# Cross attention with its scores on 64 by 64 tiles of the array, over key rows interleaved by part

## The reference

```python
x = x + _L1_xattn_ref(_layernorm(x, axis=-1), ctx_1024, ctx_1024, mask_Bx1xSxS2_bk0, ...)

def _L1_xattn_ref(queries, keys, values, mask, W_q, W_k, W_v, W_proj, b_proj):
    Q = (queries @ W_q.T).reshape(b, sq, N_HEADS, D_HEAD).transpose(0, 2, 1, 3)
    K = (keys @ W_k.T).reshape(b, -1, N_HEADS, D_HEAD).transpose(0, 2, 1, 3)
    V = (values @ W_v.T).reshape(b, -1, N_HEADS, D_HEAD).transpose(0, 2, 1, 3)
    scores = jnp.einsum('bhqd,bhkd->bhqk', Q, K) / scale
    scores = jnp.where(mask, scores, NEG_INF)
    attention = jax.nn.softmax(scores, axis=-1)
    heads_out = jnp.einsum('bhqk,bhkd->bhqd', attention, V)
    ...
    out = heads_out @ W_proj.T + b_proj
```

## Time and profile before

| | |
|---|---|
| median of 3 runs | 2487.47 us (2486.67 to 2489.14) |
| the profiled execution | 2501.07 us, span 2499.3 us, mean granted PE clock 0.971 |
| PE busy | 2236.3 us (89%) |
| DVE, ACT, POOL busy | 1650.0 (66%), 1243.2 (50%), 808.3 us (32%) |
| the stage's loop over batches: first K00, last addition of the output | 386.27, 732.00 us after the span's start |

### The profile page before, as it was taken

The page is one execution under the profiler, slowest core; times in us unless marked ns, Lnnn a source line. Parts: engine busy times, 40 slices in busy tenths (PEclk is TensorE's granted clock), DMA queues, the critical chain, the costliest instruction groups (busy, mean ns, idle before and its releaser), DMA issues. The chain is left out here.

```text
span 2499.3 us, 50978 instructions
## 1 busy us (share of the span) xinstructions
PE 2236.3 (89%) x20593; PEld 1417.7 (57%) x20650; DVE 1650.0 (66%) x3182; ACT 1243.2 (50%) x2071; POOL 808.3 (32%) x660
## 2 busy tenths in 40 slices
PE   6885779999978889999999999699879999998898
PEld 4764445666654555656655666356546555566554
DVE  4987456555548756888888854644576666665577
ACT  2326234555554225555555554566436555563565
POOL 5610052233206112321233300045445455433254
PEclk8998899999989989999999999899999999999999
DMA  3200453423313047676776764133322323220231
GB/s 113 71 7 1 144 136 103 107 78 106 79 66 106 13 118 144 121 133 133 151 146 122 125 113 80 34 102 102 116 67 67 86 69 86 69 67 23 71 96 60
DMA packets 358618, 226.84 MB, mean 91 GB/s; under 512 B 289913, under 2 KB 326610, under 8 KB 358386
## 3 DMA queue, kind: packets, MB, share of 16 engines
q1 hardware_dynamic: 355314, 215.20, 35.5%
q0 software_dynamic: 3072, 8.39, 1.2%
HBM read 114.87 MB, written 0.52 MB: 46 GB/s over the span
## 5 line engine op out<-in xcount | busy, mean ns | idle before, releaser
L3950 POOL TENSOR_TENSOR l2x_rows<-l2x_rows,l2x_one 128x256 f16<-128x256 f32 (+1 forms) x91 | 89.2, 1006 | 379.6 <-DVE l2x_rows L1507 354.5
L100 PE MATMUL PS<-hot 128*128 128x512 f16 x460 | 134.3, 427 | 82.1 <-DVE l0a_g L1119 17.5
L4054 PE MATMUL PS<-l2x_rows,l2x_pth 128*128 128x512 f16 x832 | 200.3, 379 | 1.7 <-DVE l2x_mean L4263 1.7
L3711 DVE CUSTOM_DVE_ANT_0 l1x_junk<-PS,l1x_bias 128x1024 bf16<-128x1024 f32 (+1 forms) x128 | 123.2, 991 | 73.6 <-PE PS L3371 72.7
L4256 DVE TENSOR_TENSOR l2x_pl<-l2x_sc,l2x_ph 128x1664 f16<-128x1664 f32 x64 | 125.1, 1954 | 44.6 <-ACT l2x_ph L4133 43.9
L4151 ACT ACTIVATE l2x_meanT<-PS 128x256 f32<-128x256 f32 x64 | 24.5, 383 | 250.5 <-PE PS L4016 250.5
L4241 DVE CUSTOM_DVE_ANT_0 l2x_sc<-PS,l2x_bias 128x1665 f32<-128x1665 f32 x64 | 120.9, 1889 | 36.3 <-issue 35.0
L3711 DVE CUSTOM_DVE_ANT_0 l3x_junk<-PS,l3x_bias 128x1024 bf16<-128x1024 f32 (+1 forms) x128 | 123.6, 991 | 24.3 <-PE PS L3371 21.6
L4008 PE MATMUL PS<-l2x_kh,l2x_qth 128*128 128x512 f16 (+1 forms) x512 | 131.9, 339 | 1.5 <-issue 1.5
L4008 PE MATMUL PS<-l2x_kh,l2x_qtl 128*128 128x512 f16 (+1 forms) x512 | 131.9, 339 | 0.0
L4008 PE MATMUL PS<-l2x_kl,l2x_qth 128*128 128x512 f16 (+1 forms) x512 | 131.9, 339 | 0.0
(11 more groups left out here) (866 smaller groups left out, 6109.0 us busy)
## 6 DMA issues: line engine op xcount, KB each, us to landing
l2f_unit<-in_L_ffn_units_dram SPq DMA_DIRECT2D x36, 384.0 KB, 3.1
l3f_unit<-in_L_ffn_units_dram SPq DMA_DIRECT2D x34, 384.0 KB, 3.0
l1x_kst<-l1x_kh SPq DMA_DIRECT2D x128, 100.1 KB, 2.2
l3x_kst<-l3x_kh SPq DMA_DIRECT2D x128, 100.1 KB, 2.2
l2x_rows<-in_ctx_dram SPq DMA_DIRECT2D x8, 1536.0 KB
l1x_ctx<-in_ctx_t_dram SPq DMA_DIRECT2D x7, 1601.0 KB, 7.3
l3x_ctx<-in_ctx_t_dram SPq DMA_DIRECT2D x7, 1601.0 KB, 7.0
l1x_kst<-l1x_kl SPq DMA_DIRECT2D x64, 100.1 KB, 2.2
```

The source lines that it names most:

```text
L100: self.nc.tensor.matmul(self.PS[:, bank, :], self.hot[:, 0:P], self.hot[:], start=True, stop=True)
L3711: v.tensor_tensor_reduce(junk[:, slot(it), 0:n], slot_banks(it)[:, 0:n], bias[:, 0 if normed else b % 2, at:at + n], 1.0, LOWEST, ALU.add, ...
L3950: last = nc.gpsimd.tensor_tensor(high[:, at], of[:, at], one[0:p, at].unsqueeze(2).unsqueeze(3).to_broadcast([p, i, NC, P]), ALU.mult)
L4054: nc.tensor.matmul(PS[:, ACC, :], pth[:, u % 2, m, :], rows2[:, b % 2, :, :, m, :], start=(m == 0), stop=False)
```

## The change

A second function, `row_tiled_attention`, is a copy of the first and serves l1x; l3x keeps the old one. What differs for l1x:

- **Key rows.** `kst` has 128 rows instead of 97 for a pair of heads, 64 for each head: rows x, x + 4, x + 8, ... are part x, with x = 0 a constant, 1 and 3 the high, 2 the low keys. The constant rows of both buffers are written once by two DMAs on SP (behind the loads, ahead of the mask's loads) from a row in the spare half of the value buffer; the stack DMAs write every fourth row.
- **Queries.** `qst` has one block of 64 columns for a pair instead of two with a mask: a head's queries stand in its own 64 rows. They are turned by fp16 products with an identity; the pair mask goes.
- **Scores.** `turned(b, m)` makes both banks in one pass: four mask products of 64 by 64 weights and 512 columns, for all 13 m, then 32 score products of 64 by 64 weights and 64 columns, on row half r and column half (a half of the key tile); bank r holds the heads of row half r. It waits for both exponentials of the m before, and at m = 0 for both M items. `values` reads heads 2u + g for g.
- **Mask.** `ON_VECTOR` is empty: DVE adds no mask, and POOL makes no second layout (line 3260 has no counterpart).
- **Maxima.** An A item is two pairs of heads by a quarter of the keys: four products of 401 columns (398 in the last quarter) on four 64 by 64 tiles, and two maxima of 401 on DVE. There are 16 as before. M is two transposes instead of four, and two copies of 1 by 256 on ACT instead of one of 1 by 512.
- **Order.** In the steps that hold both, A now stands ahead of V1, V2 and V3 (and A10 ahead of M0), and M1 moves to the step before the last. ACT and DVE do both exponentials of an m first, then the items of both steps (before: the items of the step before ahead of each exponential). Warm-up is three products for each A item.
- W_proj's rows are laid out for the new order of heads; the mask in columns is no longer an input.

As a diff between the old function and the new one, cut:

```diff
-    ON_VECTOR = list(range(4))
+    ON_VECTOR = list(range(4)) if normed else []
-    A = [("A", u, h) for u in range(R) for h in range(NH)]
+    A = [("A", v, j) for v in range(QV) for j in range(NCH)]
...
-                 [("V", 1, 0), A[2]], [A[3]], [P_, A[4]], [("V", 2, 0), A[5]], [A[6]], [A[7]], [("V", 3, 0), A[8]], [A[9]],
-                 [("M", 0, 0), A[10]], [A[11]], [A[12]], [A[13]], [A[14]], [A[15]], [], [("M", 1, 0)]]
+                 [A[2], ("V", 1, 0)], [A[3]], [P_, A[4]], [A[5], ("V", 2, 0)], [A[6]], [A[7]], [A[8], ("V", 3, 0)], [A[9]],
+                 [A[10], ("M", 0, 0)], [A[11]], [A[12]], [A[13]], [A[14]], [A[15]], [("M", 1, 0)], []]
...
-                for g, part in enumerate((kh, kl, kh)):
-                    sp.dma_start(kst[g * F:(g + 1) * F, b % 2, c * RC + j, :],
+                for x, part in ((1, kh), (2, kl), (3, kh)):
+                    sp.dma_start(kst[x::PARTS, b % 2, c * RC + j, :],
...
+                for a in range(2):
+                    sp.dma_start(kst[0::PARTS, a, :, :], const.unsqueeze(1).to_broadcast([F, R, NK])).then_inc(const_rows, 16)
...
-                for i, at, n in pieces(*halves[j]):
-                    last = nc.tensor.matmul(PS[:, bank + i, 0:n], qst[0:3 * F, b, c, :, :],
-                                            kst[0:3 * F, b % 2, c, at:at + n], start=True, stop=True)
+                at, n = chunks[j]
+                for i in range(2):
+                    for r in range(2):
+                        rows = slice(r * S, (r + 1) * S)
+                        last = nc.tensor.matmul(PS[i * S:(i + 1) * S, bank + r, 0:n], qst[rows, b, 2 * c + i, :],
+                                                kst[rows, b % 2, 2 * c + i, at:at + n], start=True, stop=True)
...
-                def turned(b, m, g):
+                def turned(b, m):
-                            pe.wait_ge(exp_done, e - G2 + 1)
+                            pe.wait_ge(exp_done, e)
-                        pe.wait_ge(row_made, G2 * b + g + 1)
+                        pe.wait_ge(row_made, G2 * (b + 1))
...
+                                    nc.tensor.matmul(PS[at:at + w_, S_BANK + r, :], of_bias[:, m * P + at:m * P + at + w_], one_hot[half, :],
+                                                     start=(x == 0), stop=False, skip_group_check=True)
+                    for u in range(R):
+                        for at, w_ in keys:
+                            for r in range(2):
+                                rows = slice(r * S, (r + 1) * S)
+                                last = nc.tensor.matmul(PS[at:at + w_, S_BANK + r, u * S:(u + 1) * S],
+                                                        kst[rows, b % 2, u, m * P + at:m * P + at + w_], qst[rows, b, u, :],
...
                     for m in range(KT):
+                        turned(b, m)
                         for g in range(G2):
-                            turned(b, m, g)
                             for it in at_step(b, m * G2 + g):
                                 item(it)
...
-                            for it in step_before(b, m * G2 + g):
-                                item(it)
                             exp(b, m, g)
+                        for g in range(G2):
+                            for it in at_step(b, m * G2 + g):
+                                item(it)
```

More of the change, by code:

```diff
@@ L3760, in layer_1_xattn @@
 def layer_1_xattn(k):
-    context_attention(k, "l1x", normed=False, finished=("l0x", "l0a", "l0f"))
+    row_tiled_attention(k, "l1x", normed=False, finished=("l0x", "l0a", "l0f"))
 def layer_3_xattn(k):
@@ L4369, in heads, with heads_by_half @@
         return w.reshape(2, 2, 4, D // H, D).transpose(1, 0, 2, 3, 4).reshape(2, P, D)
+    def heads_by_half(w):
+        return w.reshape(2, 4, 2, D // H, D).transpose(0, 2, 1, 3, 4).reshape(2, P, D)
     def columns(v):
@@ L4415, in laid_out @@
         a[f"L1_xattn_{name}_t"] = a.pop(f"L1_xattn_{name}").T
-    a["L1_xattn_W_proj_t_heads"] = heads(a.pop("L1_xattn_W_proj").T)
+    a["L1_xattn_W_proj_t_heads"] = heads_by_half(a.pop("L1_xattn_W_proj").T)
     both = a.pop("L2_xattn_Wkv")
@@ L4423, in laid_out @@
     a["fside_columns"] = tiled(a["fside_SxS2_0"])
-    a["mask_columns"] = tiled(a["mask_Bx1xSxS2_bk0"][:, 0])
     n = np.arange(D)
```

695 lines of the change are left out of this document (added).

## The result

The changed kernel takes 2505.65 us (median of 5, 2499.12 to 2513.92), beside 2489.14 (2486.67 to 2491.34) for the kernel before: ratio 1.0073, 95% interval 1.0057 to 1.0089. It is slower, by 16.5 us between the medians and 18 by the ratio; 2483.5 was forecast, 2502 was the upper end, and the sign is wrong.

What follows compares the result with a forecast made beforehand. It took PE as the bound, with POOL's fixed 12.0 us from V3's end to K00. Terms -4.4 - 1.9 - 0.5 + 2.9 = -3.9 us off 2487.47 gave 2483.5 (2478 to 2489; 2471 to 2502 with most rivals).

Steps and rivals of the forecast that it cites:

- the price of a score pass: PE's scores of one m: bias 0.22 us plus 8 rounds of 0.032 us, 0.48 us in all.
- T: Time of one score pass on PE: 0.48 us if four tiles run together, 0.95 if two do.
- K00 to V3's end: PE's stretch per batch: -0.82 us in three batches, -0.42 in three with O and P, -0.7 in the first; -4.4 together.
- POOL's cover: After V3, PE reaches the next batch's first T's end in 11.1 to 11.3 us, inside POOL's 12.4: cost 0.
- VectorE: DVE's maximum items: two reductions of 0.50 us, 1.0 an item against 1.15, but 16.0 a batch against 14.6.
- Way in: Up to the first K00: cheaper query turning and copies, first K00 at 384.4 instead of 386.27, -1.9 us.
- End: Last batch, values 0 to the end of values 12: 21.7 us after, 18.8 before, +2.9.
- The chain of 1.81: Last batch: score pass, both exponentials and release follow one another, so one m lasts at least 1.81 us, against 1.56.
- Rival 1: Score passes and maxima: tiles sharing columns, or their weight loads, queue; T 0.95, +27 us, so 2510; chance 0.10.
- Rival 4: Last batch: the clock falls to half, T and values double, +7 us, so 2490; chance 0.06.

Runs made afterwards that it cites:

- grouped_last_tile: The changed kernel with the last key tile's 16 score products of the 64-wide part first, then the 16 of the 1-wide part: 2490.93 us, ratio 1.0006.
- last_key_left_out: The changed kernel without the 1601st key in scores, exponentials and values, so no 1-wide products: 2494.65 us, ratio 1.0029.
- two_bank_pairs: grouped_last_tile with V1, V2, V3 ahead of A2, A5, A8, and the last batch's odd-m scores in two free banks: 2488.53 us, ratio 0.9995.

## Why the prediction was wrong

**The step that failed** is the price of a score pass. T was worked out for a tile of 128 keys and charged 13 times a batch. The words "new ones are charged" put one change of tile size, 0.11 us, to each pass; in m = 12 there are 17 more. Each costs about what was said (0.09 to 0.12), but the number was wrong, and with it the rounds (16 of two products, not 8 of four): the pass takes 2.78 us instead of 0.6. Both facts stood there: 1601 keys leave 65, and the 0.11 was read from the rows. They weren't put together, since the pass was priced from the loop's form and not once for its last turn. What the order of its products alone is worth, by the grouped kernel: 14.5 us of the stage and 15 to 17 of the time. In the profile it is 7.5 us from POOL's start to K00 (1.0 to 1.4 in each of six batches), 2.2 ahead of the last batch and 2.2 in it, 2.2 in K00 to POOL of the two batches in which the clock was lost, and 0.4 in the way in. With it gone the stage is still 1.4 us longer than before, not 3.9 shorter. The other 5.3 are the end (2.2 more than forecast), the way in (1.9), the first batch (0.6) and the stretch ahead of the last batch (0.6).

**Point by point** (what the prediction calls one step of two bias and eight score products is one m, so two steps; its sums use it rightly):
- *K00 to V3's end.* Right, nearly row by row. In the batch of 513.87 (without O and P), from start to start: K00 to values 0 8.05 (8.08 forecast), to values 1 4.15 (4.19), to values 2 3.90 (3.88), to values 4 6.67 (6.6), to values 5 5.41 (5.36), to values 6 1.71 (1.7), to POOL's release 2.89 (2.03 before, +0.85 forecast). Sum -0.74 against -0.82; -0.55 against -0.42 with O and P. The first batch gave -0.1, not -0.7.
- *POOL's cover.* Right as a bound (12.0 in grouped_last_tile and in both kernels without the last key), wrong in what hides under it: "11.1 to 11.3 us" holds only where m = 12 has no change (last_key_left_out: 11.1 in four of six batches), and with the grouped pass it is just under 12.0 (K00 waits 0.2 to 0.3 us for POOL in four batches). In the changed kernel it is 13.1 to 13.5.
- *VectorE.* Right: 1.0 us an item, idle time of PE ahead of V and A items ended by DVE's maxima.
- *Way in.* Not settled to the microsecond: 64.83 after and 64.50 before, but the two kernels with the old way in took 66.06 and 66.54, with the clock at half for other stretches (10.2 us near the start in all but before, where it is 6.8 and 3.4 more at 369; 6.8 more at 355 in those two). So it gave between +0.3 and -1.7, where -1.9 was forecast. The turning products and the copies save what was said (1.95 to 1.07, 2.72 to 1.29 us), but a cost was left out: the query's parts are now written to every fourth fp16 of a row, which DVE does at half the pace. DVE's rows of it before:

```profile
353.22 0.69 DVE L3609 TENSOR_SCALAR l1x_q_high<-l1x_xn 128x1024 f16<-128x1024 f32 x1
...
353.95 1.29 DVE L3611 CAST l1x_v<-l1x_q_high 128x1024 f32<-128x1024 f16 x2
...
355.16 1.22 DVE L3612 SCALAR_TENSOR_TENSOR l1x_v<-l1x_xn,l1x_q_high 128x1024 f32<-128x1024 f32 x1
```

and after, with PE's turning products (line 4104), DVE's copies (4454) and its first maximum (4500):

```profile
340.84 1.32 DVE L4402 TENSOR_SCALAR l1x_v<-l1x_xn 128x1024 f16<-128x1024 f32 x1
...
342.19 1.32 DVE L4403 COPY l1x_v<-l1x_v 128x1024 f16<-128x1024 f16 x1
...
343.30 2.48 DVE L4404 SCALAR_TENSOR_TENSOR l1x_v<-l1x_xn,l1x_v 128x1024 f16<-128x1024 f32 x1
...
345.85 1.07 PE L4104 MATMUL PS<-l1x_ident,l1x_v 128*128 128x128 f16 x16 [2.15 <-DVE l1x_v L4404]
...
350.02 1.06 PE L4104 MATMUL PS<-l1x_ident,l1x_v 128*128 128x128 f16 x16
...
351.12 1.29 DVE L4454 CAST l1x_qst<-PS 128x512 f16<-128x512 f32 x2 [2.88 <-PE PS L4104]
...
353.81 0.57 DVE L4500 CUSTOM_DVE_ANT_0 l1x_junk<-PS,l1x_bias 128x401 bf16<-128x401 f32 x1
```

  3.2 us (353.22 to 356.38) became 4.9 (340.84 to 345.78), the third step alone 2.48 instead of 1.22. DVE's first reduction stands 45.7 us after the stage's start, 45.8 before, not 3.1 earlier.
- *End.* +2.9 forecast, +7.2 measured, +5.1 with the grouped pass. The chain of 1.81 is right (1.86 measured), and two_bank_pairs shows that it is the chain. Left out were ACT's copy of the sums ahead of the exponentials (the first m lasts 2.23), two passes with a gap of 0.2 to 0.3 us in their stream, 0.7 for the last tile's remaining changes, and 1.0 in the tail, where the clock is at half for the output's products.
- *Rivals.* Rival 1 had the size (2510) and the wrong mechanism; its words "or their weight loads, queue" would fit only if every pass were slow. Rival 4, the clock, is right in kind but not in its cause or place. It put the loss on the thinner m of the last batch, and there the clock stayed full from 706.7 to 727.1; the stretches came around K00 and at the head of the last batch, behind the weak pass. That a pass is weak for some of its turns and not for all was no rival.

The floor of about 25 ns from start to start that the Trainium skill states ("TensorE: Matmul & The Clock Gate", section "Wait — 56ns, not 53.3ns?") does not hold between tiles: the trace has four starts in 32 ns, 3 to 4 ns apart within a round. On one tile the starts are 32 ns apart, which it allows.

## What to carry to other kernels

Price a loop's last turn by itself: write out its shapes and count the changes of tile size, for a remainder of one key can cost more than a full tile. Products on tiles of unlike size belong in groups; the order alone was worth some 15 us here. And where a second engine's fixed time covers a stretch, a gain there is worth nothing, but a loss is paid as soon as it exceeds the cover, which was under 1 us.

## What the runs showed of the hardware

- Four products on 64 by 64 tiles run together, those that share columns too (other banks, the same partitions): a round of four products of 64 columns takes 32 ns, four of 512 columns 0.23 us.
- A change between a 64-wide tile and a 1-wide one costs 0.09 to 0.12 us beyond the columns that stream (0.12 to 0.14 from start to start), and a 20-wide one about as much (2.20 us for the scores of a pass); a 40-wide tile costs nothing beside 64-wide ones.
- PE's busy share doesn't show what the clock follows. Behind passes of 2.8 us that count as busy and stream 64 columns each 0.13 us, the clock went to half for 3.4 us in two batches of six, behind two of them for 6.8 us in each of six batches. Unread products behind the weak pass didn't help; where there was none, they did. Which of like batches loses the clock stays open.
- At 68 small products and their weight loads in 1.17 us, PE stopped after every 256 instructions for up to 1.56 us, until 2.2 to 2.6 us behind the start of a 16384-byte transfer on its instruction queue. At 1.86 us for the same work such gaps are few.
- DVE took 2.48 us to write 128x1024 fp16 values to every fourth place, against 1.22 for fp32 values that lie together.
